# Two-layer graph network on one core: the last item in four short sides and two batches, a short product block moved to third place

## The chip, the cores and the metric

The kernel runs on one core of one Trainium2 chip. The core has five engines with their own instruction streams: TensorE (PE in the profile) multiplies matrices, VectorE (DVE) works element by element, ScalarE (ACT) applies functions and scales, GpSimd (POOL) issues gathers and additions to DRAM here, and SyncE (SP) issues plain transfers. They meet at semaphores. The metric is the device time of one execution in microseconds (us); lower is better.

## The reference

1250 nodes carry 512 values, 41250 edges lead from `src` to `dst` (sorted by `dst`), and each edge carries 512 values `edge_attr`. Both layers start with a layer norm and a ReLU. Layer one is a graph convolution. Layer two multiplies, for each of 64 paths, one 32-wide piece of the source's row by one piece of the edge's row, scales it, and adds it to one piece of the destination's row:

```python
def _L1_gnn_ref(x_nodes, x_edges, path_coeffs, src, dst, path_indices):
    x1 = x_nodes[src].reshape(-1, 16, 32)
    x2 = x_edges.reshape(-1, 16, 32)
    i1, i2, i3 = (path_indices[:, 0], path_indices[:, 1], path_indices[:, 2])
    contrib = path_coeffs[None, :, None] * x1[:, i1, :] * x2[:, i2, :]
    edge_out = jnp.zeros((x2.shape[0], 16, 32), x_nodes.dtype).at[:, i3, :].add(contrib)
    out = jnp.zeros((n_nodes, 512), x_nodes.dtype).at[dst].add(edge_out.reshape(-1, 512))
    return out
...
h = relu(layernorm(x)); x = x + L0_gnn(h, src, dst, W, b)
h = relu(layernorm(x)); x = x + _L1_gnn_ref(h, edge_attr_512, coeffs, src, dst, paths)
```

## The kernel before

**Layer one** (0 to about 290 us) reads the indices, counts the edges between nodes as matrices, multiplies them with the features, and stores layer two's node rows `h2_rows` in DRAM.

**Layer two** goes over the edges in tiles of 128. Seven tiles in a row are a side; each side's destinations lie within a window of 32 node rows, and four sides are an item, so that the four share TensorE's 128 output rows (`M` = 32 each). There are 12 items. A turn is one pass over an item (`item_turns`, which repeats it where destinations spread over more than 32 rows; here each item has one turn). A turn's 28 tiles are done in two batches of 14. SP loads the batch's edge rows (`load`, L311, into `x2_mem`), POOL gathers its source rows (`gather_turn`, by `indirect_dma_start` in L522, into `x1_mem`), one tile per instruction.

**The products** are VectorE's part. The paths are sorted out beforehand to 64 possible products in four blocks of 16 (`G` = 4, `PG` = 16); block 3 holds those that depend on the data (`late_products`, L738, behind branches), and with these inputs 10 of its 16 are done, 58 in all. A product (L735) takes 14 tiles at once: `q_mem` gets `x1` at one offset times `x2` at another, 448 values per partition. The offsets come from a packed word: `unpack` (L291 in the trace) splits it in registers, and every six products VectorE loads six words more (`load_pairs`, L729), at `p % CHUNK == 0`. `q_mem` is double-buffered by slot: `product_slot` (L745) of slot s first waits until TensorE has `summed` slot s-2 (L747). I number slots 0 to 3 in batch 0, 4 to 7 in batch 1; slots 3 and 7 are block 3.

**The sums** are TensorE's. `sum_slot` (L1058) multiplies a one-hot matrix of destinations (`hot_mem`, made by ACT in `destinations`) with the 16 products of the block and adds batch 0 and batch 1 of a turn in one of four PSUM banks, one per block. A block's sum is 28 records in the trace, four rounds of one tile for each of the four sides. ACT copies the finished sums to `S`, scaled by the coefficients (`save`, L898), during the next turn, and TensorE mixes them: `mix` (L1047) adds every product's sum to its place in a fifth bank, 16 products (32 records) behind each of the slots 0 to 3 of the next turn. ACT copies the result to `acc` (`save_mixed`, L914), and POOL adds it to the output, one addition for each side (`add_rows`, L518), each waiting for the one before it.

**The last item** holds what is left: two sides of 7 tiles and a third of one tile with the last 34 edges, 15 tiles in one batch (`product_last`, `sum_last`, `load_last`, `gather_last`). Both `gather_last` and half of `load_last` wait until turn 10 has multiplied its last slot. Behind its sums all 64 products of this last item are mixed and added to the output.

**The order of work** is written by hand for each engine, each working its own stream in program order. SP's `load` gives the first two sides' edge rows ahead and holds the other two back until layer one is done with the memory (`agg_summed`, `h2_stored`).

## Time and profile before

| | us |
|---|---|
| median of 3 runs | 1154.01 |
| lowest to highest | 1152.04 to 1155.46 |
| profiled execution | 1154.45 |
| its span | 1152.8 |
| layer two's regular turns, 0 to 10 | 294.4 to 1027.9 |
| the last item's first product | 1051.8 |
| the last 64 mixings | 1111.2 to 1138.7 |

The profile has one row per group of instructions: when it starts, how long it takes, and in brackets how long the engine was idle before it and what released it. An engine's name with a q (DVEq, PEq, SPq) is its sequencer, the part that reads instructions, works on registers and issues transfers. "issue" is idle time in which the engine waited for nothing that the profile shows. PEclk is the clock granted to TensorE as a share of full speed. In the lists of order below, `ISA` rows are register work and waits of a sequencer.

### The profile page before, as it was taken

Reading aid. Unit: us, or ns where it says so; the run is one execution under the profiler, and the core shown is the slowest. Engines: PE = TensorE matmul, PEld = TensorE weight load, DVE = VectorE, ACT = ScalarE, POOL = GpSimd, SP = SyncE. Lnnn points to the kernel's source line nnn. Section 1 sums busy time; section 2 is a strip of 40 time slices with the busy share of each in tenths; the row PEclk is TensorE's granted clock in tenths of the full one; section 3 lists DMA queues with packets and bytes.
Section 4 is the critical chain, followed back from the end, with each engine's and each line's share of the span. In section 5 each row is a group of like instructions: output and inputs, shape, how many; then the busy total and the mean of one; then the engine's idle time right before and its main releaser. Section 6 shows DMA issues by size and latency. Waiting matters only on the chain.

```text
span 1152.8 us, 21994 instructions
## 1 busy us (share of the span) xinstructions
PE 841.4 (73%) x5118; PEld 405.0 (35%) x5119; DVE 890.8 (77%) x1955; ACT 420.1 (36%) x1612; POOL 533.6 (46%) x610
## 2 busy tenths in 40 slices
PE   2788779990686967778696777859587785951985
PEld 1344333440341514324151432416142341510465
DVE  4667768440798989989898998989899898964600
ACT  4887886336024042332405133240513324013040
POOL 3222210435746555664656566465556656123010
PEclk9799998995887988989798898979988898985965
DMA  8000002135856556775655577575656767324000
GB/s 154 1 0 0 0 1 74 37 119 173 297 211 235 185 193 217 260 260 212 241 185 194 208 260 260 212 252 186 221 182 246 260 230 252 102 107 106 1 11 7
DMA packets 58553, 183.07 MB, mean 159 GB/s; under 512 B 19940, under 2 KB 20068, under 8 KB 52588
## 3 DMA queue, kind: packets, MB, share of 16 engines
q0 software_dynamic: 28528, 88.43, 24.4%
q1 hardware_dynamic: 21048, 88.36, 20.4%
q10 hardware_dynamic: 8900, 5.55, 1.8%
q14 instruction: 65, 0.53, 0.1%
q8 instruction: 12, 0.20, 0.1%
HBM read 173.45 MB, written 8.86 MB: 158 GB/s over the span
## 4 chain that ended last, share of the span: by engine, by line
DVE 31%; DVEq 25%; PE 20%; issue 15%; POOL 3%; ACT 2%; DMA 2%; SPq 1%; POOLq 0%; ACTq 0%
DVE q_mem L735 28%; DVEq L291 11%; DVEq L729 9%; PE psum L1067 5%; PE psum L1053 4%; PE psum L974 3%; PE psum L985 3%; PE psum L1008 2%; DVEq L735 2%; POOL x_mem L522 2%; DVE x_mem L656 1%; PE psum L999 1%; PE psum L971 1%; DMA x_mem<-in_L_gnn_W 1%; ACT hot_mem L823 1%
## 5 line engine op out<-in xcount | busy, mean ns | idle before, releaser
L735 DVE TENSOR_TENSOR q_mem<-x_mem 128x448 f32 (+1 forms) x1334 | 722.7, 622 | 104.6 <-DMA x_mem<-h_rows,src_now 55.6
L1067 PE MATMUL psum<-q_mem,hot_mem 128*32 128x512 f32 x2584 | 419.4, 719 | 206.5 <-DVE q_mem L735 193.9
L522 POOL DMA_INDIRECT x_mem<-h_rows,src_now x323 | 399.6, 1237 | 269.2 <-DVE q_mem L735 175.4
L1067 PEld LDWEIGHTS psum<-q_mem,hot_mem 128*32 128x32 f32 x2584 | 100.2, 127 | 485.5 <-issue 376.0
L1053 PEld LDWEIGHTS psum<-S,ident 128*128 128x128 f32 x1664 | 203.1, 203 | 33.3 <-issue 33.3
L1053 PE MATMUL psum<-S,ident 128*128 128x32 f32 x1664 | 208.6, 287 | 0.0
L908 ACT ACTIVATE S<-psum,coef 128x32 f32<-128x32 f32 (+1 forms) x832 | 153.1, 369 | 128.1 <-PE psum L1067 105.5
L914 ACT ACTIVATE acc<-psum 128x512 f32<-128x512 f32 x13 | 7.8, 597 | 456.7 <-PE psum L1053 391.3
L656 DVE TENSOR_SCALAR x_mem<-x_mem,spare 128x320 bf16<-128x320 f16 x324 | 79.1, 301 | 39.8 <-issue 39.8
L518 POOL DMA_DIRECT2D out<-acc x55 | 49.3, 896 | 105.7 <-ACT acc L914 82.6
L985 PE MATMUL psum<-x_mem,hot_mem 128*128 128x320 bf16 x324 | 68.4, 338 | 28.7 <-DVE x_mem L656 14.1
L823 ACT ACTIVATE hot_mem<-x_mem,spare 128x128 bf16<-128x128 f16 x232 | 72.5, 388 | 26.7 <-PE psum L985 26.3
L893 ACT ACTIVATE hot_mem<-iota_f,rel 128x32 f32<-128x32 f32 x323 | 72.1, 375 | 25.4 <-PE psum L1067 24.1
L985 PEld LDWEIGHTS psum<-x_mem,hot_mem 128*128 128x128 bf16 x324 | 33.0, 102 | 61.8 <-DVE x_mem L656 49.8
L390 POOL TENSOR_TENSOR spare<-spare 128x7 f32<-128x7 f32 (+1 forms) x48 | 15.0, 316 | 85.4 <-DVE x_mem L656 85.1
L1008 PE MATMUL psum<-x_mem 128*128 128x512 bf16 x140 | 46.5, 379 | 0.0
L974 PE MATMUL psum<-x_mem 128*128 128x512 f32 x80 | 36.4, 598 | 0.0
L827 ACT ACTIVATE hot_mem<-hot_mem 128x640 bf16<-128x640 bf16 (+1 forms) x48 | 34.5, 719 | 1.5
L1045 PE MATMUL psum<-dst_rel,iota_f 128*32 128x324 f32 x24 | 8.2, 508 | 32.5 <-DMA x_mem<-h_rows,src_now 32.5
L1008 PE MATMUL psum<-S,x_mem 128*128 128x512 bf16 x80 | 30.3, 379 | 0.0
L703 DVE TENSOR_TENSOR x_mem<-x_mem 128x512 f32<-128x512 f32 x10 | 7.0, 701 | 28.2 <-ACT x_mem L861 28.2
L643 DVE TENSOR_TENSOR q_mem<-psum,q_mem 128x320 f32 x49 | 23.7, 483 | 4.3 <-PE psum L985 4.1
(156 smaller groups left out, 399.2 us busy)
## 6 DMA issues: line engine op xcount, KB each, us to landing
x_mem<-in_edge_attr SPq DMA_DIRECT2D x44, 1024.0 KB
x_mem<-in_edge_attr SPq DMA_DIRECT2D x44, 768.0 KB
x_mem<-h_rows,src_now POOLq DMA_INDIRECT x323
x_mem<-in_edge_attr SPq DMA_DIRECT2D x2, 1792.0 KB
out<-acc POOLq DMA_DIRECT2D x55, 64.0 KB
x_mem<-in_x SPq DMA_DIRECT2D x1, 2304.0 KB
out<-x_mem ACTq DMA_DIRECT2D x9, 256.0 KB
h_rows<-x_mem ACTq DMA_DIRECT2D x9, 256.0 KB, 2.0
```

Of the source, the lines that this page charges most:

```text
L291: eng.reg_alu(r, word, base, ALU.python_mod)
L522: pool.indirect_dma_start(x1[:, t, :], None, h2_dram[:, :], bass.IndirectOffsetOnAxis(ap=now[:, t - first:t - first + 1].bitcast(u32), axis=0)
L656: nc.vector.tensor_scalar(key_hot[:, n % RING, :], iota_h, keys[:, n:n + 1], None, ALU.is_equal).then_inc(hots_ready, 1 if n + 1 < first[- ...
L729: dve.load(turning[chunk % 2], packed[0:1, at:at + CHUNK])
L735: return nc.vector.tensor_tensor(q[s % 2][:, 0:tiles, p % PG, :], x1[:, first:first + tiles, ds(a, U)], x2[:, first:first + tiles, ds(b, U ...
L823: last = nc.scalar.activation(row_hot[s % 2][:, t, :], iota_h[:, 0:P], ACT.Abs, bias=minus_row[:, ds(item * TI + (first[s] + t), 1)])
L893: last = nc.scalar.activation(hots[:, at[s] + t - cut[s][0], :], iota_f[:, :], ACT.Abs, bias=rel[:, 1, k:k + 1])
L908: last = nc.scalar.activation(S[:, p * U:(p + 1) * U], sums, ACT.Copy, scale=coef[:, p:p + 1])
L985: nc.tensor.matmul(key_sums[s % 2], row_hot[s % 2][:, t, :], key_hot[:, n % RING, :], start=(t == 0), stop=(t == sizes[s] - 1)).then_inc(h ...
L1008: last = nc.tensor.matmul(ps[agg_bank(c)], counts[:, m, c * P:(c + 1) * P], rhs[m], start=(m == 0 and rhs is features[0]), stop=(m == C - ...
L1053: last = nc.tensor.matmul(ps[MIX][:, ds(at, U)], ident, S[:, p * U:(p + 1) * U], start=False, stop=True, skip_group_check=True)
L1067: last = nc.tensor.matmul(ps[g][side * M:(side + 1) * M, :], hot[:, first + k, :], q[s % 2][:, k, :, :].rearrange("p n u -> p (n u)"), sta ...
```

## The change

**The last item** is cut in another way: 11 items are full (`FULL`), and the last has sides of 4, 4, 4 and 3 tiles (`TL`, `TR`), done in two batches of 8 and 7 tiles by the same functions as the others. Its loads and gathers have semaphores per batch (`x1_last`, `x2_last`) and wait for slots 3 and 7 of the turn before, as a regular turn's do. Indices come in four transfers per array instead of two (`by_partition`, `by_column`). The final additions to the output are four instead of three. **The block order** is now `ORDER` = 0, 1, 3, 2: block 3, the short one with branches, is third in every batch, except in the last item's second batch (`ORDER_END`). **Register loads** come behind the fourth product of six (`CHUNK // 2`), not behind the first. **ACT's saves** of blocks 2 and 3 both wait for slot 7's sum; those of the last item wait by block. **SP** loads three sides ahead in layer one (`EARLY` = 3) and no longer waits for `h2_stored`; parts of layer one's matrices have other homes in memory, with a new buffer `more`. Line numbers shift: the product is L750 after, the load L744, the wait L761, the sum L1077, the mixing L1063, the save L925.

```diff
     T = 7
     S4 = 4
     M = P // S4
     TI = S4 * T
     TB = TI // 2
-    ITEMS = -(-E // (P * TI))
-    FULL = E // (P * T)
-    TAIL = E - FULL * P * T
+    FULL = E // (P * TI)
+    ITEMS = FULL + 1
     SIDES = S4 * ITEMS
-    COLS = FULL * T + 2
-    AT_LAST = (ITEMS - 1) * TI
-    TL = 2 * T + 1
-    NORMAL, LAST_ITEM = [T, T, T, T], [T, T, 1, 1]
+    SF = S4 * FULL
+    TL = 4
+    REST = E - FULL * P * TI
+    TR, TAIL = divmod(REST - (S4 - 1) * P * TL, P)
+    AT_LAST = FULL * TI
+    AT_REST = AT_LAST + (S4 - 1) * TL
+    COLS = AT_REST + TR + 1
+    NORMAL, LAST_ITEM = [T] * S4, [TL] * (S4 - 1) + [TR + 1]
     CUT = [[(0, 4), (0, 4), (0, 3), (0, 3)], [(4, 7), (4, 7), (3, 7), (3, 7)]]
-    CUT_LAST = [(0, T), (0, T), (0, 1)]
+    CUT_LAST = [[(0, TL // 2)] * S4, [(TL // 2, n) for n in LAST_ITEM]]
     WINDOWS = N // M + 2
     G = 4
     PG = NP // G
@@ -46,6 +50,8 @@
     SURE = NP - LATE
     assert SURE > (G - 1) * PG
     TURN = 2 * G
+
+    ORDER, ORDER_END = [0, 1, 3, 2], [0, 1, 2, 3]
...
     EXACT = 256
+    EARLY = 3
...
-            sp.wait_ge(pads_set, 6)
-            sp.dma_start(dst_i[:, 0:FULL * T].rearrange("p (b t) -> p b t", t=T), dst_full).then_inc(idx_in, 16)
-            sp.dma_start(dst_i[0:TAIL, FULL * T:FULL * T + 1], dst_tail).then_inc(idx_in, 16)
+            sp.wait_ge(pads_set, 5)
+            for to, edges in zip(by_column(dst_i), by_partition(dst)):
+                sp.dma_start(to, edges).then_inc(idx_in, 16)
...
-                        if j == 0 and s == 2:
+                        if j == 0 and s == EARLY:
                             sp.wait_ge(agg_summed, C)
-                            for i in range(2):
-                                sp.wait_ge(h2_stored[i], 16 * (C // 2))
                         a, b = CUT[j][s]
                         to = x2_mem[:, (j * TB + at[s]) * D:(j * TB + at[s + 1]) * D]
                         sp.dma_start(to, edge_full[:, ds(item * S4 + s, 1), a * D:b * D].rearrange("p b n -> p (b n)")
                                      ).then_inc(x2_in[j], 16)
 
-            def load_last(turn):
-                sp.wait_ge(multiplied, group_before(turn, G - 1))
-                for s in range(2):
-                    if s:
-                        sp.wait_ge(multiplied, group_before(turn, TURN - 1))
-                    sp.dma_start(x2_mem[:, s * T * D:(s + 1) * T * D], edge_full[:, FULL - 2 + s, :]).then_inc(x2_last, 16)
-                sp.dma_start(x2[0:TAIL, 2 * T, :], edge_tail).then_inc(x2_last, 16)
+            def load_last(window, turn):
+                for j in range(2):
+                    at = tiles_before(CUT_LAST[j])
+                    sp.wait_ge(multiplied, group_before(turn, j * G + G - 1))
+                    if j:
+                        n = tiles_before(CUT_LAST[0])[-1]
+                        sp.wait_ge(x1_last[0], window * (16 * n) + 16 * n)
+                    for s in range(S4):
+                        a, b = CUT_LAST[j][s]
+                        first = j * TB + at[s]
+                        if j and s == S4 - 1:
+                            sp.dma_start(x2[0:TAIL, first, :], edge_tail).then_inc(x2_last[j], 16)
+                        else:
+                            sp.dma_start(x2_mem[:, first * D:(first + b - a) * D], edge_last[s][:, a * D:b * D]).then_inc(x2_last[j], 16)
 
...
+            def gather_turn(item, window, turn, at, cuts, landed):
+                col = item * TI
                 for j in range(2):
-                    now = src_now[:, j * TB:(j + 1) * TB]
+                    n = tiles_before(cuts[j])[-1]
                     pool.wait_ge(multiplied, group_before(turn, j * G))
-                    nc.gpsimd.tensor_copy(now, src_cols[:, ds(item * TI + j * TB, TB)]).then_inc(idx_copied, 1)
+                    pool.sem_inc(pool_steps, 1)
+                    nc.gpsimd.tensor_copy(src_now[:, j * TB:j * TB + n], src_cols[:, ds(col, n)]).then_inc(idx_copied, 1)
+                    col = col + n
                     pool.wait_ge(idx_copied, turn * 2 + j + 1)
                     pool.wait_ge(multiplied, group_before(turn, j * G + G - 1))
                     pool.sem_inc(pool_steps, 1)
-                    gather(now, range(j * TB, j * TB + TB // 2), j * TB, x1_in[j])
+                    gather(j, range(0, n // 2), landed[j])
                     add_rows(2 * j, older, turn)
-                    gather(now, range(j * TB + TB // 2, (j + 1) * TB), j * TB, x1_in[j])
+                    gather(j, range(n // 2, n), landed[j])
                     add_rows(2 * j + 1, older, turn)
                 for s in range(S4):
                     pool.reg_mov(older[s], newer[s])
                 keep_rows(pool, newer, at, window)
 
-            def gather_last(window, turn, at):
-                now = src_now[:, 0:TL]
-                for j in range(2):
-                    pool.wait_ge(multiplied, group_before(turn, j * G + G - 1))
-                nc.gpsimd.tensor_copy(now, src_cols[:, AT_LAST:AT_LAST + TL]).then_inc(idx_copied, 2)
-                pool.wait_ge(idx_copied, turn * 2 + 2)
-                pool.sem_inc(pool_steps, 1)
-                gather(now, range(TL), 0, x1_last)
-                for s in range(S4):
-                    add_rows(s, older, turn)
-                for s in range(S4):
-                    pool.reg_mov(older[s], newer[s])
-                keep_rows(pool, newer, at, window)
-
...
-            for s in range(S4 - 1):
+            for s in range(S4):
                 add_rows(s, newer, total + 1)
-            pool.wait_ge(out_added, total * (16 * S4) + (16 * (2 * S4 - 1) + 16))
+            pool.wait_ge(out_added, total * (16 * S4) + (16 * (2 * S4) + 16))
 
...
-            def product_slot(turn, s, first, tiles, done):
-                g = s % G
+            def product_slot(turn, s, block, first, tiles):
                 dve.wait_ge(summed, group(turn, s - 2))
                 dve.sem_inc(vector_steps, 1)
-                if g == G - 1:
+                if block == G - 1:
                     late_products(s, first, tiles, SURE)
-                for p in range(g * PG, min((g + 1) * PG, SURE)):
+                for p in range(block * PG, min((block + 1) * PG, SURE)):
                     last = product(s, first, tiles, p)
-                    if p < STEADY and p % CHUNK == 0:
+                    if p < STEADY and p % CHUNK == CHUNK // 2:
                         load_pairs(p // CHUNK + 1)
-                last.then_inc(multiplied, done)
+                last.then_inc(multiplied, 1)
 
             load_pairs(0)
 
@@ -760,14 +774,16 @@
                 for j in range(2):
                     dve.wait_ge(x1_in[j], turn * (16 * TB) + 16 * TB)
                     dve.wait_ge(x2_in[j], turn * (16 * S4) + 16 * S4)
-                    for g in range(G):
-                        product_slot(turn, j * G + g, j * TB, TB, 1)
+                    for g, block in enumerate(ORDER):
+                        product_slot(turn, j * G + g, block, j * TB, TB)
 
             def product_last(window, turn, at):
-                dve.wait_ge(x1_last, window * (16 * TL) + 16 * TL)
-                dve.wait_ge(x2_last, window * 48 + 48)
-                for g in range(G):
-                    product_slot(turn, g, 0, TL, 1 if g < G - 1 else 1 + G)
+                for j in range(2):
+                    n = tiles_before(CUT_LAST[j])[-1]
+                    dve.wait_ge(x1_last[j], window * (16 * n) + 16 * n)
+                    dve.wait_ge(x2_last[j], window * (16 * S4) + 16 * S4)
+                    for g, block in enumerate(ORDER if j == 0 else ORDER_END):
+                        product_slot(turn, j * G + g, block, j * TB, n)
 
...
-            def save(turn):
+                last.then_inc(a_chain1, 1)
+                act.wait_ge(a_chain1, turn * 4 + (7 + j))
+                nc.scalar.activation(hots, hots, ACT.Relu, scale=-1.0, bias=1.0).then_inc(hot_ready, 1)
+
+            def save(turn, slots_done):
+
                 act.wait_ge(mixed, turn + 1)
-                for g in range(G):
-                    act.wait_ge(summed, group_before(turn, G + g))
-                    for p in range(g * PG, (g + 1) * PG):
+                for block in range(G):
+                    act.wait_ge(summed, group_before(turn, G + slots_done[block]))
+                    for p in range(block * PG, (block + 1) * PG):
...
+            def sum_turn(item, window, turn, cuts, sizes):
+                distances(item, window, turn, sum(sizes))
                 for j in range(2):
                     act.wait_ge(summed, group_before(turn, j * G + G - 1))
-                    destinations(CUT[j], j, NORMAL, turn, 1, 1)
+                    destinations(cuts[j], j, sizes, turn)
                     if j == 0:
-                        save(turn)
+                        save(turn, [0, 1, G - 1, G - 1])
                 save_mixed(turn)
 
-            def sum_last(window, turn):
-                distances(ITEMS - 1, window, turn, TL)
-                act.wait_ge(summed, group_before(turn, TURN - 1))
-                destinations(CUT_LAST, 0, LAST_ITEM, turn, 2, 2)
-                save(turn)
-                save_mixed(turn)
-
...
-            save(total)
+            save(total, ORDER_END)
...
+            def sum_turn(turn, cuts, orders):
                 for j in range(2):
                     pe.wait_ge(hot_ready, turn * 2 + (j + 1))
-                    for g in range(G):
-                        sum_slot(turn, j * G + g, CUT[j], j * TB, j == 0, j == 1, 1)
+                    for g, block in enumerate(orders[j]):
+                        sum_slot(turn, j * G + g, block, cuts[j])
                         if j == 0:
                             if g == 0:
                                 pe.wait_ge(acc_ready, turn + 1)
                             mix(g)
 
-            def sum_last(window, turn, at):
-                pe.wait_ge(hot_ready, turn * 2 + 2)
-                for g in range(G):
-                    sum_slot(turn, g, CUT_LAST, 0, True, True, 1 if g < G - 1 else 1 + G)
-                    if g == 0:
-                        pe.wait_ge(acc_ready, turn + 1)
-                    mix(g)
-
```

VectorE, the start of a regular turn's batch 0, before. `ISA [waits summed]` is slot 0's wait, L735 a product, L291 the unpacking, L729 the register load.

```order
L762 ISA [waits x1_in0]
L747 ISA [waits x2_in0]
L291 ISA [waits summed]
L735 TENSOR_TENSOR q_mem<-x_mem 128x14x32
L729 TENSOR_LOAD packed
L291 ISA
L735 TENSOR_TENSOR q_mem<-x_mem 128x14x32
L291 ISA
L735 TENSOR_TENSOR q_mem<-x_mem 128x14x32
```

The same place after:

```order
L776 ISA [waits x1_in0]
L761 ISA [waits x2_in0]
L309 ISA [waits summed]
L750 TENSOR_TENSOR q_mem<-x_mem 128x14x32
L309 ISA
L750 TENSOR_TENSOR q_mem<-x_mem 128x14x32
L309 ISA
L750 TENSOR_TENSOR q_mem<-x_mem 128x14x32
L309 ISA
L750 TENSOR_TENSOR q_mem<-x_mem 128x14x32
L744 TENSOR_LOAD packed
L309 ISA
```

The load stands behind the fourth product, where it stood behind the first.

VectorE, the end of batch 0, before. Behind the branches of block 3 (L740) come its two unconditional products, and then batch 1's first slot:

```order
L740 UNCONDITIONAL_BRANCH
L291 ISA
L735 TENSOR_TENSOR q_mem<-x_mem 128x14x32
L291 ISA
L735 TENSOR_TENSOR q_mem<-x_mem 128x14x32
L747 REGISTER_ALU [waits x2_in1,x1_in1]
L291 ISA [waits summed]
L735 ISA
L735 TENSOR_TENSOR q_mem<-x_mem 128x14x32
```

After, at the end of the third slot (the same branches, L755) and at the end of the fourth, where batch 1 begins:

```order
L755 UNCONDITIONAL_BRANCH
L309 ISA
L750 TENSOR_TENSOR q_mem<-x_mem 128x14x32
L309 ISA
L750 TENSOR_TENSOR q_mem<-x_mem 128x14x32
L761 REGISTER_ALU
L309 ISA [waits summed]
L750 TENSOR_TENSOR q_mem<-x_mem 128x14x32
...
L750 TENSOR_TENSOR q_mem<-x_mem 128x14x32
L761 REGISTER_ALU [waits x2_in1,x1_in1]
L309 ISA [waits summed]
L750 ISA
```

A full block, with its three register loads, has moved between the short block and the end of the batch, in batch 1 too.

TensorE, the last item's last sum, then the last mixings, before. The sum of 15 tiles is followed by 16 mixings (L1053) of the turn before, of which the first stands here, and then by the wait for `acc` and the last 64:

```order
L1060 REGISTER_ALU
L1067 MATMUL psum<-q_mem,hot_mem 32x512 [waits multiplied]
L1067 MATMUL psum<-q_mem,hot_mem 32x512 x14
L291 ISA
L1053 MATMUL psum<-S,ident 128x32
...
L1093 ISA
L1096 ISA [waits acc_ready]
L1050 MATMUL psum<-zeros_b 128x512 [waits saved]
```

After, where the last item's four sums of batch 1 stand between the two:

```order
L1070 REGISTER_ALU [waits hot_ready]
L1077 MATMUL psum<-q_mem,hot_mem 32x512 [waits multiplied]
L1077 MATMUL psum<-q_mem,hot_mem 32x512 x6
L1070 REGISTER_ALU
L1077 MATMUL psum<-q_mem,hot_mem 32x512 [waits multiplied]
L1077 MATMUL psum<-q_mem,hot_mem 32x512 x6
...
L1095 ISA
L1098 ISA [waits acc_ready]
L1060 MATMUL psum<-zeros_b 128x512 [waits saved]
```

All 64 last mixings stand behind the last sum, before and after.

## Rows read from the trace of the kernel before

**Rows 1.** The page: busy time, share, instructions by engine; shares of the chain.
```profile
PE 841.4 (73%) x5118; PEld 405.0 (35%) x5119; DVE 890.8 (77%) x1955; ACT 420.1 (36%) x1612; POOL 533.6 (46%) x610
...
DVE 31%; DVEq 25%; PE 20%; issue 15%; POOL 3%; ACT 2%; DMA 2%; SPq 1%; POOLq 0%; ACTq 0%
```
**Rows 2.** Stages: start:end length, busy (count) by engine, granted clock, DMA share, GB/s.
```profile
core 0: us, PE busy (x) PEld busy (x) DVE busy (x) ACT busy (x) POOL busy (x), PEclk, DMA share, GB/s
294.40:1027.90 733.50, 557.51 (x3879) 256.52 (x3877) 689.26 (x1276) 201.03 (x973) 417.63 (x355) 0.87 0.62 217
1107.10:1138.80 31.70, 28.05 (x129) 27.48 (x129) 0.00 (x0) 11.97 (x65) 3.02 (x4) 0.50 0.08 9
```
**Rows 3.** VectorE's timeline: start, length, engine, line, form, count, [idle before, releaser].
```profile
294.37 0.63 DVE L735 TENSOR_TENSOR q_mem<-x_mem 128x448 f32 x1 [31.87 <-DMA x_mem<-h_rows,src_now]
...
829.45 0.63 DVE L735 TENSOR_TENSOR q_mem<-x_mem 128x448 f32 x1 [1.86 <-issue]
...
862.28 0.63 DVE L735 TENSOR_TENSOR q_mem<-x_mem 128x448 f32 x1 [0.48 <-PE psum L1067]
...
896.94 0.62 DVE L735 TENSOR_TENSOR q_mem<-x_mem 128x448 f32 x1 [1.84 <-issue]
...
962.56 0.62 DVE L735 TENSOR_TENSOR q_mem<-x_mem 128x448 f32 x1 [1.85 <-issue]
964.25 30.64 DVE L735 TENSOR_TENSOR q_mem<-x_mem 128x448 f32 x57 [1.07 <-issue]
...
1051.77 0.66 DVE L735 TENSOR_TENSOR q_mem<-x_mem 128x480 f32 x1 [23.77 <-DMA x_mem<-h_rows,src_now]
```
**Rows 4.** Pieces of the chain, start and length; last, L729's durations in ns (min/median/max).
```profile
956.26 0.17 DVEq L291
...
956.59 0.17 DVEq L291
...
958.31 0.17 issue
...
961.03 0.08 DVEq L772
...
964.52 0.17 DVEq L291
964.76 0.16 DVEq L291
...
L729 DVEq TENSOR_LOAD <-packed x185: 811/834/1690, 268.1 to 1075.6; - x185
```
**Rows 5.** TensorE's timeline, columns as in rows 3.
```profile
479.25 3.64 PE L1067 MATMUL psum<-q_mem,hot_mem 128*32 128x512 f32 x28 [2.97 <-issue]
...
546.92 6.56 PE L1067 MATMUL psum<-q_mem,hot_mem 128*32 128x512 f32 x28 [4.86 <-DVE q_mem L735]
...
856.50 5.32 PE L1067 MATMUL psum<-q_mem,hot_mem 128*32 128x512 f32 x28 [0.46 <-DVE q_mem L735]
...
881.18 4.12 PE L1067 MATMUL psum<-q_mem,hot_mem 128*32 128x512 f32 x24 [4.86 <-DVE q_mem L735]
...
923.98 3.63 PE L1067 MATMUL psum<-q_mem,hot_mem 128*32 128x512 f32 x28
...
978.14 3.76 PE L1053 MATMUL psum<-S,ident 128*128 128x32 f32 x32
```
**Rows 6.** SyncE's and GpSimd's timelines: an index transfer's issue, and gathers.
```profile
14.46 0.59 SPq L306 DMA_DIRECT2D spare<-in_L_gnn_path_indices  x1
...
289.90 0.95 POOL L522 DMA_INDIRECT x_mem<-h_rows,src_now  x1 [0.30 <-issue]
...
1029.17 1.05 POOL L522 DMA_INDIRECT x_mem<-h_rows,src_now  x1 [0.83 <-POOL src_now L546]
```
**Rows 7.** ScalarE's timeline: the save of a block.
```profile
966.54 2.95 ACT L908 ACTIVATE S<-psum,coef 128x32 f32<-128x32 f32 x16 [2.80 <-remote]
```
**Rows 8.** TensorE's and GpSimd's timelines and a stretch, the last mixings and additions.
```profile
1111.20 27.52 PE L1053 MATMUL psum<-S,ident 128*128 128x32 f32 x128
...
1112.00:1138.00 26.00, 26.00 (x124) 26.00 (x123) 0.00 (x0) 7.14 (x41) 1.96 (x3) 0.50 0.07 9
...
1146.30 0.76 POOL L518 DMA_DIRECT2D out<-acc  x1 [2.28 <-DMA out<-acc]
```

138 lines of the change are left out of this document (71 added, 67 removed).

## The prediction

> **What bounds the kernel now.** I read the busy table and the shares of the chain first [rows 1]. VectorE is busy 890.8 us and heads the chain with 31%, but "DVEq", the part of VectorE that reads its instructions, has 25%: in places VectorE waits for its own instruction stream. The stages come next. Layer two's eleven regular turns fill 294.4 to 1027.9 us [rows 2], VectorE then stands for 23.8 us [rows 3], the last item follows, the last 64 mixing matmuls run at a granted clock of 0.50 [rows 2], and the tail after 1138.8 is additions to the output. TensorE's clock has two levels, 1.2 and 2.4 GHz; 0.50 is the lower.
>
> I call the four product blocks of a batch slots 0 to 3 (batch 0) and 4 to 7 (batch 1), and count from a turn's first product. VectorE's timeline [rows 3] gives the period: turn 0 starts at 294.37, turn 10 at 962.56, so a turn takes 66.82 us on average, in two kinds: 65.6 (from 896.94) and 67.5 (from 829.45). The 58 products of a batch need 31.3 (0.62 and 30.64). Idle times make the rest: 1.8 before a turn, 1.1 behind a batch's first product, and, in the long turns, 0.5 before batch 1 (862.28), put down to TensorE.
>
> The instruction stream explains them [rows 4]. In batch 0 the unpacking of a product's offsets starts every 0.24 us (964.52, 964.76), in batch 1 every 0.33 (956.26, 956.59), against 0.54 for a product. A register load (L729) costs 0.81 to 1.69 us. From the last unpacking (957.6, one pitch behind the last but two) to the next turn's first product (962.56) pass about 4.9, of which 2.7 (958.31 to 961.03) lie at the jump back. And the next turn begins at a fixed distance from one event: TensorE has summed slot 2 at 856.50 + 5.32 = 861.8, and the turn starts 35.1 later; or at 923.98 + 3.63 = 927.6, and it starts 35.0 later [rows 3, 5]. That wait lets VectorE into batch 1, and 35.1 is what the stream then needs: 58 x 0.33 = 19.3, the way to the next turn 4.9, and 10.9 for eight loads and the branches. Slot 2's end plus 35.1 is the turn, and TensorE's two speeds are the two kinds of turn.
>
> **The change, part by part.**
> *Start.* Two more index transfers on SP and on ACT. The issue of a short one takes 0.59 us on SP [rows 6], and W's transfer queues behind two: +1.0 (0 to +2.3). The last item's counting has 15 tiles for 16: -0.5 (-1.5 to +1.0). The third side's edge rows and the dropped wait bring nothing, since the first product waits for the last gathered row: issued at 289.90, first product at 294.37, and POOL issues one per 1.25 us (0.95 and 0.30 idle) whatever SP does [rows 3, 6]. Sum +0.5.
>
> *Regular turns, batch 0.* The load now follows the fourth product, so the 1.1 us behind the first one shrinks to about 0.2. Slot 0 is multiplied at 9.0. TensorE sums it in 5.4, mixes 3.8, sums slot 1 in 3.6, mixes 3.8 and finds the short block long multiplied: summed at 29.2, or at 30.9 to 31.3 at the lower clock [rows 5]. Before, slot 2 was summed at 30.7 or 32.4 (861.8 and 927.6 less their turns' starts). That is the gain meant: 1.1 to 1.5 a turn.
>
> *Batch 1.* What this gain meets: slot 7 is now a full block with three loads, and may enter the stream only when slot 5 is summed, since it overwrites its buffer. Queued behind that wait is all that VectorE has left of the turn. Before, a full block (16 x 0.54 = 8.6) hid this sum; now only the short one (10 x 0.54 = 5.4) does. Batch 0 ends at 31.3, so slot 5 is multiplied at 31.3 + 2 x 8.6 = 48.4. TensorE stands 4.9 us before it; after such a pause the sum took 6.56 or about 5 (881.18: 24 of the 28 records in 4.12), and after a pause of 3.0 only 3.64 [rows 5]. I take 5.1: released at 53.5. From there 16 x 0.33, three loads of 1.0, and 4.9 to the next turn are 13.2: the next turn at 66.7. The old bound (29.7 + 35.1) would give 64.8. If slot 2 is summed late (31.3), batch 1 starts drained: 67.9. ACT now saves two blocks, 2.95 us each, after slot 7's sum, the second behind a pause of 2.8 [rows 7]: slot 7 is multiplied at 62.4, summed by 67.7, saved by 73.6 to 76.4, while slot 0's sum asks for it at 66.7 + 9.0 = 75.7: 0 to +0.7. I take 67.4, between 66.7 and 68.6, with 65.5 if slot 5 is summed at full clock and ACT is in time. Ten periods: 674 for 668.2, **+5.8**.
>
> *Into the last item.* Before: 962.56 to 1051.77, 89.2 us, since gathers began only at 1029.17, when turn 10 had multiplied everything [rows 3, 6]. Now eight tiles are gathered behind slot 3 as in any turn (8 x 1.25 us on POOL, with some 30 us to spare), and no jump back comes: released at 53.5, + 8.5 for the stream of slot 7, + about 2.5 = 64.5. **-24.7**. With that cover gone it would cost the old 24.
>
> *Last item.* From 15 tiles in 58 products to 8 and 7 tiles in 116. One tile more took a product from 0.62 to 0.66 [rows 3], so 8 tiles take 0.3 to 0.4: less than unpacking and loads together. The stream sets it: 58 x 0.24 + 9.2 for loads + 1 = 24.1, then 58 x 0.33 + 9.2 + 1.7 = 30.0, and 2 us of waits for slots 1 and 2: 56 us. A sum is two rounds of four tiles where a regular one has four, 1.8 us at full clock or 3.3 at the lower one (half of 3.63 and of 6.56). Then the end: slot 7's sum 3.3, start 0.6, 64 mixings. ACT saves by block now, but TensorE's order still holds all 64 behind slot 7's sum; they cost 27.5 as before [rows 8], since nothing dense runs beside them. The tail took 1152.8 - 1138.7 = 14.1 with three additions; the fourth side's is one more, 0.76 + 2.28 [rows 8]: 17.1. 56 + 3.3 + 0.6 + 27.5 + 17.1 = 104.5, against 1152.8 - 1051.8 = 101.0. **+3.5**.
>
> Sum: +0.5 + 5.8 - 24.7 + 3.5 = -14.9: a span of 1137.9. The profiled execution took 1154.45 with its span of 1152.8, so 1139.6; it lies 0.4 above the median of 1154.01, within the runs' 3.4. **1140 us.**
>
> On the clock, the trace first: between 1112 and 1138 us TensorE has a record of mixing in every microsecond, and the granted clock is 0.50; 128 matmul records take 27.52, where the 32 of a block in a turn take 3.76, 15 for four blocks [rows 5, 8]. The Trainium skill (TensorE: Matmul & The Clock Gate, What's actually happening) says that the throttled clock is the default and that sustained activity releases it. By that rule the last mixings, their saves now done ahead, would run at full clock. The measurement decides against it for a stretch that comes from idling; sums right ahead might carry a full clock over.
>
> **The rivals.**
> *A. The regular turn gains as meant.* Slot 5 is summed at full clock, or its wait is short: 65.5 a turn, 19 under my sum: 1121. For it: after 3.0 us of pause the sum took 3.64 [rows 5]. Against: the pause is now 4.9. 0.15.
> *B. Slower.* Place: the wait for slot 5 in batch 1, and the late saves, at every turn. If that sum takes 6.6, as it did once after 4.9, and slot 2 is late as well, a turn is 69.3: 10 x 1.9 = +19, 1159. It decides from 68.9 a turn on, where it has eaten the 14.9. 0.11.
> *C. The last item runs at the lower clock.* Its sums are only 1.8 us between mixings. All at the lower level, batch 0 is four times (3.3 + 6.9, a quarter of 27.5) = 41, against 24 of stream; slot 5 waits for slot 3, slot 6 for slot 4, and the item takes 68 for 56: +12, 1152. Within 0.3%. 0.13.
> *D. The last mixings run at the turns' speed.* 15 for 27.5: 1127.5. The row of 0.50 speaks against it; what speaks for it is that sums come right before. 0.03. It is what the rule above would give.
> *E. The transfers do not come early.* The last item's edge rows and gathers queue behind slots 3 and 7 as in regular turns, in which VectorE waits for a landing at turn 0 alone [rows 3]. Inside the forecast.
>
> **How the numbers follow.** The forecast holds 0.58; its own range is 1132 to 1149 (a turn of 66.7 to 68.1, 3 us for the tail). The range of all reaches from 1127 (most of A left out) to 1157 (B left out). A measurement of this kernel tells 0.3%, 3.5 us, from no change: faster is under 1150.5, slower over 1157.5. Faster 0.58 + 0.15 + 0.03 + 0.01 = 0.77, same 0.12, slower 0.11.
>
> **What would show it.** VectorE: the 1.1 us behind a batch's first product gone, and the 1.8 before a turn grown to about 4, because the stream is late; if it stays 1.8 with turns of 65.5, it is A. The 23.8 us gap gone, two batches of 24 and 30 us in its place. TensorE: slot 2 summed by 29 to 31, the last 64 mixings 27.5 us. Four additions at the end. I am wrong if turns stay 66.8 with no gap at slot 7, or if the last item is far from 56.

## The result: 5 to 8% slower, for a cost that the prediction did not have

The changed kernel took 1250.99 us (median of 4 runs, 1233.86 to 1279.12) beside 1153.83 for the kernel before (1152.04 to 1155.46). Two more runs of it took 1215.87 and 1199.40; the comparison of fast runs rests on these two alone and gives a ratio of 1.047 (95% interval 1.034 to 1.059), where the medians give 1.084. It is slower by either. Only one execution has a trace, the slowest, so how much of the spread is the effect described below is not shown. I had forecast 1140.

The page and the groups of the changed kernel (profiled execution 1279.12 us, span 1277.4), line, engine, operation, count, then busy time, mean ns, idle time and what ended it:

```profile
PE 860.0 (67%) x5111; PEld 415.9 (33%) x5118; DVE 897.2 (70%) x2018; ACT 420.1 (33%) x1616; POOL 718.0 (56%) x611
...
PE 34%; issue 21%; DVE 16%; DVEq 13%; POOL 5%; DMA 3%; ACT 3%; another core or an unknown queue 3%; SPq 1%; POOLq 0%; ACTq 0%
...
L750 DVE TENSOR_TENSOR q_mem<-x_mem 128x448 f32 (+2 forms) x1392 | 730.1, 600 | 235.1 <-DMA x_mem<-h_rows,src_now 172.1 <-PE psum L1077 31.0 <-issue 30.6
L545 POOL DMA_INDIRECT x_mem<-h_rows,src_now x323 | 585.0, 1811 | 256.4 <-DVE q_mem L750 157.2 <-issue 94.0 <-POOL src_now L554 3.5
```

Against [rows 1] GpSimd (POOL) is 184 us busier with the same 323 gathers, and VectorE now waits 172 us for gathered rows. The stages (columns as in rows 2) from the first turn's start, through turn 10, the last item, its last mixings and the tail:

```profile
core 0: us, PE busy (x) PEld busy (x) DVE busy (x) ACT busy (x) POOL busy (x), PEclk, DMA share, GB/s
295.30:1094.80 799.50, 521.61 (x3554) 237.60 (x3552) 626.95 (x1161) 196.81 (x964) 569.99 (x341) 0.80 0.55 188
1094.80:1160.10 65.30, 45.78 (x329) 22.19 (x333) 62.80 (x117) 11.17 (x52) 41.70 (x27) 0.84 0.53 181
1160.10:1232.50 72.40, 59.11 (x278) 31.05 (x270) 40.36 (x116) 17.37 (x92) 12.40 (x13) 0.57 0.19 54
1232.50:1260.00 27.50, 27.50 (x129) 27.38 (x128) 0.00 (x0) 2.57 (x15) 0.00 (x0) 0.50 0.00 1
```

Span against span: start 295.3 - 294.4 = +0.9; ten periods 799.5 - 668.2 = +131.3; turn 10 to the last item 65.3 - 89.2 = -23.9; last item to the end 117.3 - 101.0 = +16.3. Together +124.6, all that there is. The loss lies in the regular turns. Two of the ten held no gather for long and took 68.2 us; ten such would be 682, so the held gathers cost about 118 us of this execution. One of the long turns, VectorE and then GpSimd:

```profile
471.48 36.49 DVE L750 TENSOR_TENSOR q_mem<-x_mem 128x448 f32 x68
529.77 2.23 DVE L750 TENSOR_TENSOR q_mem<-x_mem 128x448 f32 x4 [21.80 <-DMA x_mem<-h_rows,src_now]
...
477.73 31.16 POOL L545 DMA_INDIRECT x_mem<-h_rows,src_now  x1 [15.06 <-DVE q_mem L750]
509.20 0.97 POOL L545 DMA_INDIRECT x_mem<-h_rows,src_now  x1 [0.31 <-issue]
```

The first gather of a batch takes 31.16 us where others take about 1. It ends at 508.89, 0.92 us after VectorE's train of products ends (507.97; the row shows its last 68, started without a pause between them). The other 13 gathers and the landing follow, and VectorE stands 21.80 us. Nine gathers in this execution took more than 5 us: four of 31.2, four of 22.6, one of 11.4.

### The profile page after: what moved, and what is told of

Read it like the earlier page. It is cut to its first block, busy times and chain, and to the rows that moved or that the text cites. A ratio compares the mean times of both kernels' runs of the same rounds, so it can differ in the third digit from the quotient of the medians.

```text
span 1277.4 us, 22215 instructions
## 1 busy us (share of the span) xinstructions
PE 860.0 (67%) x5111; PEld 415.9 (33%) x5118; DVE 897.2 (70%) x2018; ACT 420.1 (33%) x1616; POOL 718.0 (56%) x611
## 4 chain that ended last, share of the span: by engine, by line
PE 34%; issue 21%; DVE 16%; DVEq 13%; POOL 5%; DMA 3%; ACT 3%; another core or an unknown queue 3%; SPq 1%; POOLq 0%; ACTq 0%
PE psum L1077 14%; DVE q_mem L750 13%; PE psum L1063 11%; DVEq L309 5%; DVEq L744 5%; POOL x_mem L545 4%; PE psum L984 2%; PE psum L995 2%; PE psum L1018 2%; DVE x_mem L671 2%; DMA x_mem<-h_rows,src_now 2%; ACT S L925 1%; PE psum L1009 1%; DVEq L750 1%
## 5 line engine op out<-in xcount | busy, mean ns | idle before, releaser
L750 DVE TENSOR_TENSOR q_mem<-x_mem 128x448 f32 (+2 forms) x1392 | 730.1, 600 | 235.1 <-DMA x_mem<-h_rows,src_now 172.1
L545 POOL DMA_INDIRECT x_mem<-h_rows,src_now x323 | 585.0, 1811 | 256.4 <-DVE q_mem L750 157.2
L1077 PE MATMUL psum<-q_mem,hot_mem 128*32 128x512 f32 x2584 | 428.1, 751 | 310.7 <-DVE q_mem L750 286.9
L1077 PEld LDWEIGHTS psum<-q_mem,hot_mem 128*32 128x32 f32 x2584 | 99.3, 131 | 592.8 <-issue 429.9
L1063 PEld LDWEIGHTS psum<-S,ident 128*128 128x128 f32 x1664 | 215.0, 213 | 36.0 <-issue 36.0
L1063 PE MATMUL psum<-S,ident 128*128 128x32 f32 x1664 | 220.6, 296 | 0.0
L925 ACT ACTIVATE S<-psum,coef 128x32 f32<-128x32 f32 (+1 forms) x832 | 151.7, 379 | 207.3 <-issue 93.0
L839 ACT ACTIVATE hot_mem<-x_mem,spare 128x128 bf16<-128x128 f16 x235 | 73.4, 388 | 23.8 <-PE psum L995 23.3
L412 POOL TENSOR_TENSOR spare<-spare 128x7 f32<-128x7 f32 (+2 forms) x48 | 13.5, 284 | 87.9 <-DVE x_mem L671 87.6
L995 PEld LDWEIGHTS psum<-x_mem,hot_mem 128*128 128x128 bf16 x323 | 32.9, 102 | 61.1 <-DVE x_mem L671 49.5
L1018 PE MATMUL psum<-x_mem 128*128 128x512 bf16 x117 | 39.8, 379 | 0.1
L843 ACT ACTIVATE hot_mem<-hot_mem 128x640 bf16<-128x640 bf16 (+2 forms) x48 | 34.8, 725 | 1.5
L1055 PE MATMUL psum<-dst_rel,iota_f 128*32 128x323 f32 x24 | 8.3, 513 | 32.7 <-DMA x_mem<-h_rows,src_now 32.7
```

The costliest lines, as they stand in the source:

```text
L545: pool.indirect_dma_start(x1[:, j * TB + t, :], None, h2_dram[:, :], bass.IndirectOffsetOnAxis(ap=now, axis=0)).then_inc(landed, 16)
L750: return nc.vector.tensor_tensor(q[s % 2][:, 0:tiles, p % PG, :], x1[:, first:first + tiles, ds(a, U)], x2[:, first:first + tiles, ds(b, U ...
L839: last = nc.scalar.activation(row_hot[s % 2][:, t, :], iota_h[:, 0:P], ACT.Abs, bias=minus_row[:, ds(item * TI + (first[s] + t), 1)])
L925: last = nc.scalar.activation(S[:, p * U:(p + 1) * U], sums, ACT.Copy, scale=coef[:, p:p + 1])
L995: nc.tensor.matmul(key_sums[s % 2], row_hot[s % 2][:, t, :], key_hot[:, n % RING, :], start=(t == 0), stop=(t == sizes[s] - 1)).then_inc(h ...
L1018: last = nc.tensor.matmul(ps[agg_bank(c)], counts[:, m, c * P:(c + 1) * P], rhs[m], start=(m == 0 and rhs is features[0]), stop=(m == C - ...
```

## Experiments: what holds the gather

**Theory G**: a gather that meets a long train of VectorE products without a pause is held until a pause comes; behind the first product of a batch, and in small pauses later, the old place of the register loads gave such pauses. **Rival O**: the block order or the new transfers do it. Two kernels move the loads' place alone, a third the order alone.

e1, the changed kernel with the loads at their old place:

```diff
-                    if p < STEADY and p % CHUNK == CHUNK // 2:
+                    if p < STEADY and p % CHUNK == 0:
```

> The changed kernel with one edit: the register loads stand again behind the first product of six (p % 6 == 0), as before; block order, last item and all else stay changed. In the changed kernel nine first gathers of a batch took 11.4 to 31.2 us each and ended about 0.9 us after VectorE's products had paused. Theory G (gap): the 1.1 us pause of VectorE behind a batch's first product is what lets GpSimd's first gather of a batch through. It expects no gather over 3 us and a time near my forecast, 1130 to 1145. Rival O (order): the long gathers come from the new block order or from the edge loads and the last item; it expects gathers of 11 to 31 us again and 1190 or more.

e2 makes the opposite edit in the kernel before:

> The kernel before with one edit: the register loads behind the fourth product of six (p % 6 == 3). Theory G (gap) expects first gathers of a batch that take 8 to 31 us in most turns, and 1180 to 1280. Rival O (order) expects no gather over 3 us and 1145 to 1155.

e4 is the changed kernel with `ORDER = [0, 1, 2, 3]`:

> The changed kernel with the block order 0, 1, 2, 3 in all batches; loads stay behind the fourth product. Theory G (gap) expects first gathers of 8 to 31 us again, over 1170. Rival O (order) expects none over 3 us and 1125 to 1145.

Measured: e1 1171.39 us (ratio 1.019, 1.011 to 1.026), e2 1203.30 (1.042, 1.034 to 1.049), e4 1190.02 (1.034, 1.028 to 1.039). The gathers of e1 and of e2, and one place in e2:

```profile
L545 POOL DMA_INDIRECT x_mem<-h_rows,src_now x323 | 390.1, 1208 | 344.7 <-DVE q_mem L750 251.8 <-issue 90.9 <-POOL src_now L554 0.9
```

```profile
L522 POOL DMA_INDIRECT x_mem<-h_rows,src_now x323 | 520.3, 1611 | 215.5 <-DVE q_mem L735 112.6 <-issue 92.1 <-POOL src_now L530 9.6
...
482.46 0.89 POOL L518 DMA_DIRECT2D out<-acc  x1 [0.95 <-ACT acc L914]
483.65 14.56 POOL L522 DMA_INDIRECT x_mem<-h_rows,src_now  x1 [0.30 <-issue]
```

In e1, with the loads at the old place, no gather is over 2.7 us; in the kernel before, moving them alone is enough to lose 4%. So the loads' place is the cause, in either kernel, and O falls. The order still has a part in which gather is held and for how long: in e2 all ten held ones are the eighth of their batch, behind the first addition to the output (nine of 13.2 to 14.6 us, one of 22.4), not the first as I had expected; in e4 it is the eighth seven times, the first twice, and once the last item's, behind the addition there. e1 missed its own expected time (1130 to 1145) by 26 us: the lost gathers are not the only loss. That is the next section.

How a hold ends is shown in all traces. In the fifteen with two SBUF inputs, the kernels before and after among them, 129 gathers took over 1.7 us. Each was the first of a batch or one behind an addition, 119 of them ended 0.92 to 0.94 us after the first pause of VectorE since their start, down to a pause of 0.03 us, and the other ten ended without one. How a gather escapes in e1 is not shown, and it is not by a pause. Its eleven first gathers behind slot 3 pass in 1.18 to 1.20 us with the next pause about 6 us away, for example:

```profile
470.44 1.20 POOL L545 DMA_INDIRECT x_mem<-h_rows,src_now  x1 [12.93 <-DVE q_mem L750]
...
460.97 34.46 DVE L750 TENSOR_TENSOR q_mem<-x_mem 128x448 f32 x63 [0.82 <-PE psum L1077]
```

(The row runs over pauses of 0.1 us.) For these gathers the first half of theory G, that a pause of the loads lets them through, is thus not what e1 shows.

**What the train shares with the gather.** e3 leaves the edge rows out of the products: the second factor comes from a PSUM bank, so that VectorE has one input in SBUF instead of two (and one offset less to work out):

```diff
                 return nc.vector.tensor_tensor(q[s % 2][:, 0:tiles, p % PG, :], x1[:, first:first + tiles, ds(a, U)],
-                                               x2[:, first:first + tiles, ds(b, U)], ALU.mult)
+                                               ps[7][:, 0:tiles * U].rearrange("p (t u) -> p t u", u=U), ALU.mult)
```

> The changed kernel, but each product of layer two takes its second factor from a PSUM bank instead of the edge rows in SBUF (this factor is left out of the computation; edge rows are still loaded). Theory P (port): VectorE's products, with both inputs in SBUF, keep a path into SBUF busy that the gather needs as well; it expects no gather over 3 us although VectorE pauses nowhere, and 1120 to 1160. Rival Q: what holds the gather back is not on the side of VectorE's inputs (GpSimd's own waits, its queue, the memory's traffic); it expects gathers of 11 to 31 us again.

Measured 1134.73 us. Its gathers and products:

```profile
L545 POOL DMA_INDIRECT x_mem<-h_rows,src_now x323 | 312.7, 968 | 346.0 <-DVE q_mem L750 253.0 <-issue 91.2 <-DMA out<-acc 0.9
L750 DVE TENSOR_TENSOR q_mem<-x_mem,psum 128x448 f32<-128x448 f32 (+2 forms) x1392 | 722.5, 593 | 103.3 <-PE psum L1077 35.5 <-issue 32.4 <-DMA x_mem<-h_rows,src_now 32.1
```

The trains are nearly as long (up to 56 products in 29.8 us, for 72 in 38.6) and as dense (a start every 0.531 us, for 0.535), and yet no gather takes more than 1.19 us; even the usual 1.30 of a gather beside products is gone (mean 968 ns for 1237 before). So the second SBUF input is what it takes to hold a gather. The Trainium skill (SBUF — State Buffer, Who interferes with whom) says that a VectorE instruction with two SBUF inputs contends with a GpSimd instruction that reads SBUF; the trace agrees, as far as e3 tells. The Trainium skill (SBUF — State Buffer, Summary: rules for kernel authors) also says that the one that issues second is blocked until the other's instruction finishes; here a wait of 31.16 us went over some 58 products of 0.535 us. The measurement decides.

**How long is held.** e6 gives the changed kernel one short pause in each slot:

```diff
                     last = product(s, first, tiles, p)
+                    if p == min(block * PG + 8, SURE - 2):
+                        last.then_inc(paused, 1)
+                        dve.wait_ge(paused, group_before(turn, s))
```

> The changed kernel with one VectorE wait in every slot: after the ninth product of blocks 0 to 2 (the first sure one of block 3) VectorE waits until that product is done; nothing else differs. Theory G (a train of products with no pause holds the gather back) expects gathers of at most 10 us (the longest train is one block), no long wait of VectorE for gathers, and some 0.2 x 8 us more per turn than with one SBUF input: 1134.7 + 11 x 1.6 = 1152, between 1140 and 1170. The rival, that a gather's start is held back by something other than the train, expects gathers of 22 to 31 us and 1190 or more.

```profile
406.17 4.93 POOL L546 DMA_INDIRECT x_mem<-h_rows,src_now  x1 [18.94 <-DVE q_mem L751]
...
403.67 6.51 DVE L751 TENSOR_TENSOR q_mem<-x_mem 128x448 f32 x12
410.52 0.62 DVE L751 TENSOR_TENSOR q_mem<-x_mem 128x448 f32 x1 [0.34 <-DVE q_mem L751]
```

The train ends at 410.18, the gather at 411.10, again 0.92 later: a pause of 0.34 us frees it. No gather is over 4.93 us, so on the gather G is right. On the time I was wrong by 77 us: 1228.92. VectorE has 90.8 us of "issue" idle, three times that of the changed kernel, and 28.3 at the pauses themselves. I read this so, without a run that shows it: a wait for its own product also stops the instruction stream, which then starts without its lead in front of the engine, eight times a turn. The cure costs about what it saves.

**Which pauses count.** e14 (built on e10 below) keeps the load behind the first product for the first six products of a batch only:

> e10_last_mixed_early (order 0, 1, 2, 3) with the load behind the first product for the first six of a batch only, and behind the fourth for all later ones. If the pause behind the batch's first product is all that the gathers need, none is over 3 us and the time is e10's, 1122 to 1130. If each later pause matters too, the first gather of a batch passes but the eighth, behind the first addition to the output, is held as in e2: gathers of about 14.6 us in most turns, and 1160 to 1185.

1196.59 us. The first gathers pass, the eighth is held as in e2, at 406.56 for 20.15 us:

```profile
405.37 0.89 POOL L540 DMA_DIRECT2D out<-acc  x1 [0.73 <-ACT acc L931]
406.56 20.15 POOL L545 DMA_INDIRECT x_mem<-h_rows,src_now  x1 [0.30 <-issue]
```

So the loads' place later in the batch matters as much. The kernel before had shown it, in rows that the prediction does not have: its eighth gather, GpSimd and then VectorE:

```profile
340.69 2.02 POOL L522 DMA_INDIRECT x_mem<-h_rows,src_now  x1 [0.30 <-issue]
...
342.01 4.37 DVE L735 TENSOR_TENSOR q_mem<-x_mem 128x448 f32 x8 [0.23 <-issue]
```

It took double the usual time and ended at 342.71, 0.93 after VectorE paused for 0.23 us at 341.78. The pause was the loads': a register load ran from 339.98 to 340.71, just ahead of it. Four more eighth gathers there took 2.10 to 2.73 us and ended the same way.

**Does the moment of asking matter?** e8 and e9 let the first gather of a batch start later by empty semaphore steps:

```diff
                     pool.sem_inc(pool_steps, 1)
+                    for i in range(6):      # 2 in e8
+                        pool.sem_inc(pool_steps, 1)
```

> The changed kernel with two empty semaphore steps more on GpSimd between its wait for slot 3 or 7 and the batch's first gather (a delay of an estimated 0.1 us). In the changed kernel this gather always starts 0.28 us after the end of one of VectorE's products when it is held back (12 of 12), while gathers that start 0.44 us after one (12 of 14 elsewhere in the queue) take 1.06 us. Theory H (phase): at one phase against VectorE's train of products, 0.535 us apart, the gather misses every opening; another start lets it through. It expects other phases and few or no gathers over 5 us, 1130 to 1160. The rival, that any first gather is held back while the train runs, expects 22 and 31 us as before, and 1195 to 1280.

> The same with six empty steps (an estimated 0.3 us). Theory H expects the start at about 0.05 us after a product's end, where the gathers in the middle of the queue run in 1.30 us, and none over 5 us; 1130 to 1160. The rival expects gathers of 22 and 31 us and 1195 to 1280.

Profiled once each, gathers over 5 us fell from nine to five (1179.66 us) and to two (1180.21); with the same six steps e11 and e12 below have nine and eight. The starts moved from 0.28 us behind the end of a product to 0.44 (e8) and to 0.21 (e9), where 0.05 was expected. But theory H falls. Two first gathers of e9, whose starts behind a product's end agree to 0.01 us, and the pause that follows the second:

```profile
328.85 22.13 POOL L545 DMA_INDIRECT x_mem<-h_rows,src_now  x1 [11.74 <-issue]
...
405.83 1.78 POOL L545 DMA_INDIRECT x_mem<-h_rows,src_now  x1 [10.35 <-issue]
...
407.03 3.30 DVE L752 TENSOR_TENSOR q_mem<-x_mem 128x448 f32 x6 [0.34 <-issue]
```

All eleven first gathers behind slot 3 in e9, and ten of the eleven in e8, ended 0.92 or 0.93 us after VectorE's next pause; most were short (1.79 and 2.10 us) because a pause, behind the fourth product of batch 1, came 0.86 or 1.17 us after their start. In the changed kernel itself it is so in three of eleven (2.25 us); in the other eight VectorE ran over that place without a pause. So neither start lets the gather through, one case in e8 aside; what changed is how often a pause comes in time, and that the empty steps did this is not shown by one trace each. What stays open is why the same start of 0.28 us passes inside a train in e1 and is held in the changed kernel.

## Experiments: what the rest of the change is worth

**Theory S**: the short block standing third costs batch 1 of each turn through the wait for slot 5. e5 has e1's loads and the old order, each block saved after its slot; only the last item and the start are left of the change:

```diff
-    ORDER, ORDER_END = [0, 1, 3, 2], [0, 1, 2, 3]
+    ORDER, ORDER_END = [0, 1, 2, 3], [0, 1, 2, 3]
...
-                        save(turn, [0, 1, G - 1, G - 1])
+                        save(turn, [0, 1, 2, 3])
```

> The changed kernel with loads behind the first product, as in e1_loads_first, and besides the block order 0, 1, 2, 3 in all batches and each block saved after its own slot's sum: of the change only the last item in two batches, the index transfers and the edge rows ahead are left. In e1 regular turns took 68.3 to 71.9 us, and the last item 112 to the end against 101 before. Theory S (slot 5): these longer turns come from the short block standing third, since batch 1 then waits for slot 5's sum. It expects turns of 65.6 to 67.6, and 1.7 - 22 + 11.4 = 9 us less than before, 1144. The rival, that the last item's early transfers or the start slow the regular turns, expects turns of 68 and more and 1160 to 1170.

1133.30 us, ratio 0.984 (0.980 to 0.988): 1.6% faster than before, and 11 us less than I had expected, because the last item took 105.0 us to the end and not e1's 112.5. Its turns take 65.9 to 67.7, e1's 68.2 to 71.9. Between e1 and e5, which differ in the order and its saves alone, lie 38 us: by the traces 24 in the ten turns, 4 on the way into the last item, 7 in the last item, and 3 at the start, where the order has no part.

In three of e1's turns (71.5 to 71.9) slot 5 is not the step. TensorE first, then VectorE:

```profile
374.85 6.60 PE L1077 MATMUL psum<-q_mem,hot_mem 128*32 128x512 f32 x28 [6.69 <-DVE q_mem L750]
...
386.33 5.98 PE L1077 MATMUL psum<-q_mem,hot_mem 128*32 128x512 f32 x28
...
392.68 34.46 DVE L750 TENSOR_TENSOR q_mem<-x_mem 128x448 f32 x63 [4.04 <-PE psum L1077]
```

Slots 0 and 1 are summed slowly there (6.60 and 5.98 us, in the next turn 4.98 and 5.32), and VectorE stands 4.04 us before the fourth slot, where it stands 0.8 in most of e1's other turns: with the short block third, this wait for slot 1 is no longer hidden either.

In e9 a turn free of long holds shows the step at slot 5, first VectorE, then TensorE (the row at 627.30 is slots 5 and 6):

```profile
577.67 2.23 DVE L752 TENSOR_TENSOR q_mem<-x_mem 128x448 f32 x4 [3.48 <-issue]
...
611.76 6.51 DVE L752 TENSOR_TENSOR q_mem<-x_mem 128x448 f32 x12 [0.48 <-issue]
618.57 14.03 DVE L752 TENSOR_TENSOR q_mem<-x_mem 128x448 f32 x26 [0.30 <-issue]
633.10 1.16 DVE L752 TENSOR_TENSOR q_mem<-x_mem 128x448 f32 x2 [0.50 <-PE psum L1079]
...
603.18 5.32 PE L1079 MATMUL psum<-q_mem,hot_mem 128*32 128x512 f32 x28
627.30 8.99 PE L1079 MATMUL psum<-q_mem,hot_mem 128*32 128x512 f32 x56 [4.29 <-DVE q_mem L752]
```

TensorE stands 4.29 us, then slot 5's sum runs from 627.30 to 632.6, and slot 7 begins at 633.10. Three loads and the way to the next turn follow. The turn, begun at 577.67, takes 68.2, and the 1.8 us idle before a turn [rows 3] have become 3.5: the stream is late.

e7 asks whether the two batches are needed at all. It is the kernel before, with 14 of the last item's 15 tiles gathered after slot 3 of turn 10:

```diff
                 for j in range(2):
+                    first, end = (0, TB) if j == 0 else (TB, TL)
                     pool.wait_ge(multiplied, group_before(turn, j * G + G - 1))
-                nc.gpsimd.tensor_copy(now, src_cols[:, AT_LAST:AT_LAST + TL]).then_inc(idx_copied, 2)
...
-                gather(now, range(TL), 0, x1_last)
+                    gather(now, range(first, (first + end) // 2), 0, x1_last)
+                    add_rows(2 * j, older, turn)
...
```

> The kernel before with its last item as it was (15 tiles, one batch), but 14 of its 15 tiles gathered, and both large edge loads issued, once turn 10 has multiplied slot 3; the tile of the tail follows slot 7. The 23.8 us in which VectorE stood before the last item should shrink to one gather after slot 7: 1.05 and about 3.5 of landing, some 5 to 6 us. Expected 18 us less than before, 1136 (1133 to 1140); the last item itself 101 us to the end, as before. If something else holds the last item (edge rows, ScalarE's destinations), it saves less than 10 us.

```profile
1034.30 0.66 DVE L737 TENSOR_TENSOR q_mem<-x_mem 128x480 f32 x1 [7.01 <-DMA x_mem<-h_rows,src_now]
...
1046.50 8.29 PE L1069 MATMUL psum<-q_mem,hot_mem 128*32 128x512 f32 x30 [15.51 <-ACT S L910]
...
1034.30:1100.10 65.80, 50.02 (x249) 23.66 (x249) 33.33 (x58) 15.49 (x85) 0.76 (x1) 0.73 0.01 2
```

The same stretch of the kernel before:

```profile
1051.80:1110.60 58.80, 44.81 (x249) 22.25 (x249) 33.31 (x58) 3.81 (x22) 3.05 (x4) 0.79 0.04 5
```

1145.96 us, ratio 0.993 (0.990 to 0.996): 7 to 9 us less, of 18 expected. VectorE's stand shrank from 23.8 to 7.0 us as meant, but the last item then took 108.0 us to the end for 101.0. TensorE is 5.2 us longer busy with the same work at a clock of 0.73 for 0.79, and its first sum now waits for ScalarE's saves of turn 10, which the long gap had hidden.

e10 is e5 with TensorE's last mixings spread over the last item's second batch:

```diff
                         sum_slot(turn, j * G + g, block, cuts[j])
+                        if ends and j and g:
+                            mix_last(turn, g - 1)
```

> e5_last_item_only, but in the last item's second batch TensorE mixes blocks 0, 1 and 2 of that item behind the sums of slots 5, 6 and 7 instead of all 64 behind slot 7's sum (this holds for a last item of one turn). In e5 TensorE stood about 6 us before slot 6's sum and 1 us before slot 7's. If the last item is bound by TensorE at its lower clock, this time is filled: 5 to 7 us less than e5 (1133), 1127. If VectorE's stream sets the end (slots 6 and 7 wait for the sums that now come later), it gains under 2 us.

1127.46 us, ratio 0.977 (0.961 to 0.992). The last item to the end takes 99.3 us for e5's 105.0, as expected. TensorE's rows at the end of e10, and then e5's stretch of 64 mixings with its granted clock of 0.57:

```profile
1089.51 3.64 PE L1077 MATMUL psum<-q_mem,hot_mem 128*32 128x512 f32 x14
1093.08 3.93 PE L1063 MATMUL psum<-S,ident 128*128 128x32 f32 x32
1096.94 3.46 PE L1077 MATMUL psum<-q_mem,hot_mem 128*32 128x512 f32 x14
1100.33 11.00 PE L1063 MATMUL psum<-S,ident 128*128 128x32 f32 x64
```

```profile
1090.20:1114.80 24.60, 24.60 (x129) 24.48 (x128) 0.00 (x0) 2.78 (x16) 0.00 (x0) 0.57 0.00 1
```

The block behind slot 5, mixed at 1082.55, took 7.04 us, the next 3.93, the last two 11.00 together. The 64 of e5 begin fast (3.95 us for the first block, granted clock 0.95) and fall back (6.9 each, 0.50); at 0.50 throughout they took 27.5 [rows 8].

e11 puts the short block third in batch 0 alone, on e10, with loads fourth and six empty steps; e12 is the same with the old order.

> Built on e10_last_mixed_early, with loads behind the fourth product and six empty steps before the first gather (as in e9), and the short block third in batch 0 alone; in batch 1 the order is 0, 1, 2, 3 and each block is saved after its own slot. In e9, with the short block third in both batches, a turn without a held gather took 68.2 us: slot 5 multiplied at 49.5, summed at 55.0, slot 7 begun at 55.4. Theory S (slot 5): the short block third in batch 1 costs the turn, that in batch 0 gains. It expects slot 2 summed at 30.9, turns of 30.9 + 35.1 = 66.0, and 9 us less than e10's 1127 where no gather is held: 1118 to 1125. The rival, that the gain in batch 0 is eaten before batch 1 (slot 4 waits for its data or slot 2's sum comes no earlier), expects turns of 66.8 and more, 1127 or above.

> The same as e11 with the order 0, 1, 2, 3 in both batches. Theory S expects slot 2 summed at 30.7 to 31.5 (0.9 earlier than in e10 by the load's move) and turns of 66.0 to 66.6, so e11 and e12 differ by less than 5 us. If a first gather is held, times rise by 10 to 20 us per case in either.

e11 took 1315.40 us, e12 1174.38. In e11 nine gathers were held 30.7 us each:

```profile
485.28 30.70 POOL L545 DMA_INDIRECT x_mem<-h_rows,src_now  x1 [14.46 <-issue]
...
476.41 38.64 DVE L752 TENSOR_TENSOR q_mem<-x_mem 128x448 f32 x72 [0.17 <-issue]
536.72 2.23 DVE L752 TENSOR_TENSOR q_mem<-x_mem 128x448 f32 x4 [21.67 <-DMA x_mem<-h_rows,src_now]
```

The train ends at 515.05, the gather at 515.98. Its two turns without a held gather took 65.9 and 65.8 us, as theory S said, and were worth nothing. Both runs missed what was expected of them (1118 to 1125, and less than 5 us between them). e13 brings the loads' pauses back:

> e10_last_mixed_early with the short block third in batch 0 alone; loads behind the first product. Theory G expects no gather over 3 us. Theory S expects slot 2 summed at 31.5 as in e1 and turns of 31.5 + 35.1 = 66.6, against 66.9 on average in e10: 1121 to 1127, at most 3 us better than e10. The rival, that the gather queued behind the third slot meets VectorE's train at a worse moment in this order (as in e11, 30.7 us nine times), expects gathers of 20 to 31 us and over 1170.

Four of five runs took 1120.06 to 1128.83 us (ratio 0.973, 0.969 to 0.977); the fifth, the profiled one, 1178.38, and in it three gathers are held 31.2 us and two 7.1, where theory G had expected none over 3. The loads stand first and yet give no pause here:

```profile
460.51 31.17 POOL L545 DMA_INDIRECT x_mem<-h_rows,src_now  x1 [10.41 <-DVE q_mem L750]
...
429.07 61.68 DVE L750 TENSOR_TENSOR q_mem<-x_mem 128x448 f32 x115 [1.08 <-issue]
```

VectorE does 115 products, behind the first of the turn, without a pause, and the gather ends 0.93 us after the last. The old place of the loads is thus no safeguard by itself; I take it, without a run that shows it, that it gives pauses only where the instruction stream has no lead. The turns without a hold of 31 us take 65.5 to 66.9, on average 66.1 against e10's 66.7, from one trace each: the gain of the short block in batch 0 is small. I would take e10: 2.3% faster than before (interval 0.8 to 3.9), none of its four runs over 1133.46, and no gather over 2.7 us in the profiled one; four runs do not exclude a case like e13's fifth. (Its `mix_last` holds for a last item of one turn.)

## The prediction, step by step

**What failed** is a step whose cost for the gathers was put at nothing: the load "now follows the fourth product, so the 1.1 us behind the first one shrinks to about 0.2". That was booked as pure gain, beside "POOL issues one per 1.25 us whatever SP does" and "some 30 us to spare". I asked what SP might do to the gathers, and never what VectorE might. I had read VectorE's pauses as waste of its own. Where a gather is held, the next one of them is what ends the hold. Rival E, "the transfers do not come early", was put inside the forecast because VectorE had never waited for a landing after turn 0; that row described a kernel with the pauses. No rival had the gathers held, and B, my case for slower, had the wrong place. Undone by itself (e1), this edit gives back 80 us of the changed kernel's median, or 36 against the two runs that took 1215.87 and 1199.40. In the profiled execution the held gathers are about 118 of the 139 us by which it missed the forecast; the rest is 8 in the turns, 13 in the last item and 1 on the way into it and at the start.

**Regular turns without held gathers** were forecast at 67.4 (66.7 to 68.6) and took 68.2 in e9 and in the two such turns of the changed kernel. Slot 2 was summed at 30.9 (forecast 29.2 to 31.3), slot 5 multiplied at 49.5 (48.4) and summed at 55.0 (53.5), then 13.2 to the next turn (13.2). The mechanism is right and 0.8 us too short: I let VectorE's batch 1 start without a delay, but slot 2's sum took its slower kind in each turn, and a start of batch 1 without instructions read ahead cost 1.1. The late saves, 0 to +0.7, cost nothing in e9: saved 8.7 to 8.9 us into the turn, asked for at 9.1. But in two turns of the changed kernel slot 0's sum began only at 11.6 and 11.7, right behind the last save, and in its last item 4.8 us late (multiplied at 1166.9, saves until 1171.65, sum from 1171.70). A wait that the prediction did not have is VectorE's for slot 1 before the fourth slot, which made three of e1's turns 3.3 us longer.

**Into the last item**, -24.7: measured -23.9 in the changed kernel, -24.8 in e5.

**The last item**: 104.5 forecast, 105.0 in e5, but by other terms. VectorE's last product came at 61 instead of 56, and the last mixings took 24.6 for 27.5. In the changed kernel it was 117.3: slot 7 multiplied at 68.3, with mixings of 7.04 us between the sums. That is rival C, whose sum said 68, though not C's cause alone: the late saves held slot 0's sum there for 4.8 us. The fourth addition came as priced (tail 17.4 for 17.1).

**Start**: +0.9 for +0.5. Without its regular turns my sum is 0.5 - 24.7 + 3.5 = -20.7; e5's span is 20.6 below the one before, which is partly luck: by terms it is -1.3 at the start, +1.5 in the turns, -24.8 and +4.1. e3, with the whole change in it and no gather held, took 1134.7, inside my range. That is no credit to the forecast, and the 116 us between e3 and the changed kernel are not the price of the held gathers alone: e3 also unpacks one offset less, 0.05 us of the sequencer per product for 0.17.

**The clock**: rival D was given 0.03. In e5 the last mixings begin behind a sum at full clock (1.00), run their first block at 0.95 and the other three at 0.50: 24.6 us. In e10 the four blocks took 7.0 + 3.9 + 11.0. The plain row of 0.50 does not tell this. Nor does the rule of the Trainium skill (TensorE: Matmul & The Clock Gate, What's actually happening) that sustained activity releases the clock: the mixings keep TensorE busy in every record and still do not hold it.

## What to carry to other kernels

Before closing an engine's pauses, look at who works beside it: here pauses of 0.03 to 1.1 us, which looked like VectorE's loss, were what ended a gather's wait. A row that is longer than its neighbours and ends a fixed time behind another engine's pause (2.02 for 1.30, 0.93 behind) is the sign to search for, in the trace of before. And a change of several parts is measured part by part: here the last item gave 19 us (e5), the order and its saves took some 35 (e1 against e5, less the start), the loads' place between 36 and 80.

## What the runs showed of the hardware

A gather issued by GpSimd beside a dense train of VectorE products with two SBUF inputs can be held for the whole train, up to 31.2 us. Of 129 gathers over 1.7 us in fifteen traces, 119 ended 0.92 to 0.94 us after VectorE's first pause, the shortest of them 0.03 us; the usual overlap of 0.08 us between products is as a rule not enough, though ten ended without a pause. With one SBUF input none was held (1.19 us at most, e3). Gathers queued close behind one another pass through the same train in about 1.30 us each; all 129 were first of a batch or behind an addition. Why some of these pass in 1.2 us inside a train (e1) and others do not stays open.

Mixings that fill TensorE's record do not keep its clock: in e5 the first block took 3.95 us at a granted clock of 0.95, the others 6.9 at 0.50. The sums between them do not settle it either: right behind a sum of 3.64 us at 0.50 a block took 3.93 us in e10 and 7.04 in the changed kernel's last item.
